# Attention inside an adaLN block: values in batches of two key blocks, a ring of twelve buffers, the maximum stream five ticks earlier, looser waits between additions

## The chip, the cores and the metric

The kernel runs on one core of a Trainium2 chip. The time is that of one execution on the device, in microseconds (us). The engines are PE (TensorE, with its weight loads as PEld), DVE (VectorE), ACT (ScalarE), POOL (GpSimd) and SP (which issues the transfers).

## The reference

Four sequences of 1024 tokens with 1024 features go through one transformer block with modulation. In float32 throughout:

```python
h = _layernorm(x) * (1 + ca) + sa
x = x + ga * attention(h, Wq, Wk, Wv, Wo)      # 32 query heads, 8 key/value heads of 32, RoPE, causal
h = _layernorm(x) * (1 + cb) + sb
x = x + gb * (h @ W.T + bias + lora(h))        # 8 LoRA pairs of rank 16, weighted
```

The change is in the attention alone: for each head, `softmax(q k^T / sqrt(32))` with a causal mask, times v.

## The kernel before

The program has four stages after one another: the modulation vectors, the projections to q, k and v (stored to HBM), the attention, and the second half (output projection, residual, norm, linear layer with LoRA folded into the weights). The attention stage runs from about 711 us to 2092 us.

**Groups.** The attention works on 32 groups (4 sequences times 8 key/value heads, `NG`), each with 4 query heads. For a group PE computes the scores twice. The first time (`max_scores`) they stand with the query on the partition, in 38 units (`MAX_UNITS`, `NM`), and DVE takes the negated row maximum of each (`take_max`). When all 38 are there, DVE joins and splits them into a high and a low part (`split_max`: L806, L811, L813), PE transposes the result (`turn`, L920), ACT copies it, and SP writes the rows by DMA below the query vectors in `q_stack`. So the second scores (`scores`) come out with the maximum already subtracted, with the key on the partition, in 20 units (`EXP_UNITS`, `NE`). ACT takes the exponential of each (`exp`, L756). The unit of key block 0 goes into `p_sum`, the others go into one of the buffers of a ring (`p_ring`).

**Quads.** One or two units hold one block of 128 keys for all four heads: a quad, of which a group has 12, four of them in half 0 (queries 0 to 511) and eight in half 1. `values(n, q)` multiplies the quad of probabilities by v on PE. It uses a quarter of the array for each head, and the four matmuls, one per head, run side by side (the trace counts each as two).

**Sums.** POOL adds the ring buffers into `p_sum` in place (`add`, L851; 15 additions in a group, `POOL_ADDS`: four in half 0, eleven in half 1). The first addition of a half may begin once the values of its first quad are done (`FIRST_QUAD`), since those matmuls read `p_sum` themselves. PE then sums `p_sum` over the partitions (`sums`, L930 and L935), which waits for the additions of its half.

**The order.** `group_steps` writes the order of all engines by hand, in 20 ticks for a group: each tick has one unit of scores, two or three max units of the next group (38 within ticks 0 to 15, by `max_ticks`), and a quad of values two ticks after its last unit (`LAG`). The turn is at tick 17, the sums of half 0 at tick 12, those of half 1 at tick 6 of the next group. Every engine goes through the same list in order.

**Buffers.** The max units, turns and sums share three banks of PSUM (`MS`, `wait_bank`): each waits until the third before it has been taken. The scores have two buffers (`SS`), the values one (`ctx_ps`). An exponential into a ring buffer waits until the probabilities that lay there have been used by the values and by the addition (8 buffers before).

Two lines of `add` set what an addition waits for besides its probabilities:

```python
pool.wait_ge(s_pv.sem, s_pv.at(NQ * n + FIRST_QUAD[hf] + 1))
if place:
    pool.wait_ge(s_ap.sem, s_ap.at(place))      # the addition just before
```

Of the kernel before, what the change touches and what calls it, by code (L numbers as in the profile page):

```python
# [35 lines left out]
NG = B * KV  # L36
# [10 lines left out]
EXP_UNITS = []  # L47
# [6 lines left out]
NE = len(EXP_UNITS)  # L54
# [11 lines left out]
POOL_ADDS = [u for u in RING_UNITS if u not in VECTOR_ADDS + TAIL[0] + TAIL[1]]  # L66
NV, NP = len(VECTOR_ADDS), len(POOL_ADDS)
# [12 lines left out]
NM = len(MAX_UNITS)  # L80
WIDE = [i for i in range(TT) if P * (i + 1) > HALF]

RING = 8
BATCH = 1
QS = 3
SS, MS = 2, 3
LAG = 2
SUM_AT = {1: 6, 0: 12}
TURN_AT = 17


def max_ticks():

    ticks, left = [[] for _ in range(NE)], list(range(NM))
    for t in range(NE):
        for _ in range(2 if t < 10 else 3):
            if left and t < TURN_AT:
                ticks[t].append(left.pop(0))
    assert not left
    return ticks  # L100


MAX_TICKS = max_ticks()


def group_steps(n):


    steps = []
    for u in range(NE):  # L110
        if n < NG:
            steps.append(("scores", n, u))
        if n + 1 < NG:
            steps += [("max", n + 1, m) for m in MAX_TICKS[u]]
        for hf in range(2):
            at = n - 1 if hf else n
            if u == SUM_AT[hf] and 0 <= at < NG:
                steps.append(("sum", at, hf))
        if n + 1 < NG and u == TURN_AT:
            steps.append(("turn", n + 1))  # L120
        at, v = (n, u - LAG) if u >= LAG else (n - 1, u - LAG + NE)
        if 0 <= at < NG and v == QUADS[QUAD_OF[v]][-1] and QUAD_OF[v] % BATCH == BATCH - 1:
            steps += [("values", at, q) for q in range(QUAD_OF[v] - BATCH + 1, QUAD_OF[v] + 1)]
    return steps


STEPS = [("max", 0, m) for m in range(NM)] + [("turn", 0)] + [s for n in range(NG + 1) for s in group_steps(n)]
SMALL = [s for s in STEPS if s[0] in ("max", "turn", "sum")]
BANK = {s: i % MS for i, s in enumerate(SMALL)}
BEFORE = {s: SMALL[i - MS] if i >= MS else None for i, s in enumerate(SMALL)}  # L130
# [474 lines left out]
def attention(nc, consts, qk_in, v_in, ctx_out, sums_out):  # L605


    with ExitStack() as ctx:
        def sb(name, shape, dt=F32):
            return ctx.enter_context(nc.sbuf_tensor(name, shape, dt))  # L610
# [4 lines left out]
        acc = sb("p_sum", [P, 2, 2, G, HALF])  # L615
        ring = sb("p_ring", [P, RING, 2 * HALF])
        cf = sb("ctx_raw", [P, 2, HALF])
# [14 lines left out]
        def count(name, step=1):  # L632
            return Count(nc, ctx, name, step)
# [8 lines left out]
        s_av, s_ap = count("probs_added_dve"), count("probs_added_pool")  # L642
# [4 lines left out]
        def ring_place(g, u):  # L647

            r = NR * g + RING_UNITS.index(u)
            before = r - RING  # L650
            return r % RING, None if before < 0 else (before // NR, RING_UNITS[before % NR])

        def probs(g, u):

            hf, j, hs, lo, n = EXP_UNITS[u]
            if j == 0:
                return acc[:, g % 2, hf, hs[0]:hs[-1] + 1, :]
            v = ring[:, ring_place(g, u)[0], :]
            if n > 256:
                return v.rearrange("p (h n) -> p h n", h=2)[:, :, 0:n]  # L660
            return v[:, 0:G * n].rearrange("p (h n) -> p h n", h=G)
# [14 lines left out]
        def _(sp):  # L676
            def load_v(b):
                if b >= 2:
                    sp.wait_ge(s_pv.sem, s_pv.at(NQ * KV * (b - 1)))
                sp.dma_start(V[:, b % 2, :, :], v_in[b].rearrange("(i p) d -> p i d", p=P)).then_inc(s_v[b % 2].sem, 16)  # L680
# [31 lines left out]
            load_v(0)  # L712
            for step in STEPS:
                kind, n = step[0], step[1]
# [16 lines left out]
        def _(act):  # L731
# [45 lines left out]

            for step in STEPS:
                kind, n = step[0], step[1]
# [10 lines left out]
        def _(dve):  # L790
# [34 lines left out]

            for step in STEPS:
                kind, n = step[0], step[1]
# [9 lines left out]
        @block.gpsimd  # L837
        def _(pool):
            nc.gpsimd.memset(ks[MHI:MHI + DH, :, :].bitcast(F32), 1.0).then_inc(init.sem, 1)

            def add(n, u):
                hf, j, hs, lo, w = EXP_UNITS[u]
                place = NP * n + POOL_ADDS.index(u)
                pool.wait_ge(s_ex.sem, s_ex.at(NE * n + u + 1))
                pool.wait_ge(s_pv.sem, s_pv.at(NQ * n + FIRST_QUAD[hf] + 1))
                if place:
                    pool.wait_ge(s_ap.sem, s_ap.at(place))
                if hs[-1] == G - 1 and VECTOR_DONE[hf]:
                    pool.wait_ge(s_av.sem, s_av.at(NV * n + VECTOR_DONE[hf]))
                a = acc[:, n % 2, hf, hs[0]:hs[-1] + 1, lo - hf * HALF:HALF]  # L850
                nc.gpsimd.tensor_tensor(a, a, probs(n, u), ALU.add).then_inc(s_ap.sem, 1)  # L851

            for step in STEPS:
                if step[0] == "values":
                    for u in QUADS[step[2]]:
                        if u in POOL_ADDS:
                            add(step[1], u)

        @block.tensor
        def _(pe):  # L860
# [77 lines left out]

            for step in STEPS:
                kind, n = step[0], step[1]  # L940
# [455 lines left out]
```

## Time and profile before

| | |
|---|---|
| median of 3 runs | 2926.89 us (2926.59 to 2929.13) |
| the profiled execution | 2926.28 us, span 2924.5 us |
| PE busy over the span | 2654.2 us (91%) |
| POOL, DVE, ACT busy | 1669.8, 1641.4, 1024.9 us |
| turn of group 1 to turn of group 31 | 781.71 to 2045.47 us |

The span is the time between the first and the last instruction in the trace; the execution's own time is 1.8 us more. A row of the timeline gives start, duration, engine, line and operation, and in brackets how long the engine was idle before it and what released it. The granted clock ("PEclk") is a share of 2.4 GHz: 1.00 is 2.4 GHz, 0.50 is 1.2 GHz. Durations of matmuls include the way through the array, so what one costs is best read from the start of one row to the start of the next.

### The profile page before, as it was taken

The numbers are of one execution on the slowest core, as the hardware profiler recorded it, in microseconds if no ns is written. First come the engines' busy times: TensorE is split into PE (matmuls) and PEld (weight loads), VectorE is DVE, ScalarE is ACT, GpSimd is POOL, SyncE is SP. The second block draws the span as 40 slices with busy tenths as digits, with TensorE's granted clock in tenths as the row PEclk, the third lists the DMA queues.
The fourth block names the chain that finished last, engine by engine and source line by source line (L and its number), as shares of the span: only waits on it lengthen the run. The fifth ranks groups of instructions, "written<-read, shape, count | busy, mean of one in ns | idle before, by whom it ended". The sixth has DMA issues, their size and how long they took to land. (4 is left out here: it accounts for less than half of the span.)

```text
span 2924.5 us, 37728 instructions
## 1 busy us (share of the span) xinstructions
PE 2654.2 (91%) x14588; PEld 1891.7 (65%) x14588; DVE 1641.4 (56%) x2483; ACT 1024.9 (35%) x1320; POOL 1669.8 (57%) x869
## 2 busy tenths in 40 slices
PE   2599999997999999999999999999559999999998
PEld 0378888885555555555555555555358878888887
DVE  2466666655566666665665666566134545455553
ACT  0333333321445545554554445444321111111111
POOL 0443333331577778777877877777515555455543
PEclk8799999997799999999999999999779999999999
DMA  9433333324222222222132212220252333333330
GB/s 347 143 128 113 115 112 109 112 80 126 63 66 58 70 67 54 70 70 67 45 80 70 67 40 70 70 61 18 77 173 80 94 109 95 100 108 94 108 97 34
DMA packets 178696, 267.55 MB, mean 91 GB/s; under 512 B 12197, under 2 KB 105509, under 8 KB 178393
## 3 DMA queue, kind: packets, MB, share of 16 engines
q1 hardware_dynamic: 178520, 265.13, 30.8%
q8 instruction: 120, 1.97, 0.3%
q14 instruction: 56, 0.45, 0.1%
HBM read 183.19 MB, written 80.84 MB: 90 GB/s over the span
## 5 line engine op out<-in xcount | busy, mean ns | idle before, releaser
L851 POOL TENSOR_TENSOR p_sum<-p_sum,p_ring 128x1024 f32<-128x1024 f32 (+2 forms) x480 | 1033.0, 2152 | 354.4 <-PE ctx_ps L912 284.3
L800 DVE TENSOR_REDUCE neg_max<-scores_q 128x1 f32<-128x512 f32 (+3 forms) x1216 | 729.8, 656 | 512.9 <-PE scores_q L894 327.3
L756 ACT ACTIVATE p_ring<-scores 128x1024 f32<-128x1024 f32 (+2 forms) x512 | 459.3, 917 | 405.4 <-PE scores L880 282.6
L894 PE MATMUL scores_q<-k_stack,q_stack 96*128 96x512 f32 (+3 forms) x1536 | 472.7, 387 | 4.1
L876 PE MATMUL scores<-q_stack,k_stack 98*128 98x512 f32 (+1 forms) x1216 | 438.8, 439 | 5.0 <-DMA q_stack<-neg_max_rows 4.9
L876 PEld LDWEIGHTS scores<-q_stack,k_stack 98*128 98x128 f32 x1216 | 197.4, 196 | 302.1 <-issue 172.2
L894 PEld LDWEIGHTS scores_q<-k_stack,q_stack 96*128 96x128 f32 x1536 | 281.1, 195 | 74.0 <-DVE neg_max L800 45.3
L579 PE MATMUL proj_ps<-h_hi,w_hi 128*128 128x512 f32 x768 | 304.8, 397 | 1.5 <-POOL h_lo L529 1.5
L579 PE MATMUL proj_ps<-h_hi,w_lo 128*128 128x512 f32 x768 | 300.3, 391 | 0.0
L579 PE MATMUL proj_ps<-h_lo,w_hi 128*128 128x512 f32 x768 | 300.1, 391 | 0.0
L536 POOL TENSOR_TENSOR roped_hilo<-roped_hilo 128x512 fp32r<-128x512 f32 x80 | 104.1, 1302 | 333.3 <-ACT roped_hilo L418 333.3
L912 PE MATMUL ctx_ps<-p_ring,v 128*32 128x512 f32 (+3 forms) x2560 | 280.7, 513 | 0.0
L1261 POOL TENSOR_TENSOR h_scaled<-h_scaled,mod_now 128x512 f32<-128x512 f32 x64 | 65.4, 1042 | 351.8 <-DVE h_scaled L1215 351.8
L1286 PE MATMUL po<-wo_hi,ctx_hi 128*128 128x512 f32 x512 | 204.1, 399 | 5.6 <-DVE wo_lo L1206 5.6
L1327 PE MATMUL pf<-we_hi,h_hi 128*128 128x512 f32 x512 | 200.4, 391 | 5.8 <-POOL h_lo L1265 5.8
L1286 PE MATMUL po<-wo_lo,ctx_hi 128*128 128x512 f32 x512 | 200.9, 392 | 0.0
L1286 PE MATMUL po<-wo_hi,ctx_lo 128*128 128x512 f32 x512 | 200.7, 392 | 0.0
L1327 PE MATMUL pf<-we_lo,h_hi 128*128 128x512 f32 x512 | 200.2, 391 | 0.0
L1327 PE MATMUL pf<-we_hi,h_lo 128*128 128x512 f32 x512 | 200.2, 391 | 0.0
L756 ACT ACTIVATE p_sum<-scores 128x1024 f32<-128x1024 f32 x128 | 131.0, 1024 | 142.3 <-PE scores L880 82.1
L898 PE MATMUL scores_q<-mask_q_k,ident_r 128*128 128x128 f32 x768 | 174.6, 227 | 0.0
L406 ACT COPY proj_raw<-proj_ps 128x512 f32<-128x512 f32 x96 | 56.2, 586 | 333.4 <-PE proj_ps L579 333.4
(130 smaller groups left out, 3844.9 us busy)
## 6 DMA issues: line engine op xcount, KB each, us to landing
q_stack<-qk_t SPq DMA_DIRECT2D x96, 512.0 KB, 6.9
qk_t<-roped_hilo SPq DMA_DIRECT2D x80, 512.0 KB, 2.8
wm<-in_L_wmod SPq DMA_DIRECT2D x12, 2048.0 KB, 19.9
x_in<-in_L_attn_resid SPq DMA_DIRECT2D x32, 512.0 KB, 6.4
ctx_t<-ctx_raw SPq DMA_DIRECT2D x64, 256.0 KB, 2.0
ctx_tile<-ctx_t SPq DMA_DIRECT2D x32, 512.0 KB, 4.0
inv_sums<-inv_t SPq DMA_DIRECT2D x128, 128.0 KB, 5.4
x_tile<-in_L_attn_resid SPq DMA_DIRECT2D x32, 512.0 KB, 3.3
```

Source lines behind the costliest of these rows:

```text
L536: nc.gpsimd.tensor_tensor(lo, lo.bitcast(F32), qst[r % QST][:, 0, :].bitcast(F32), ALU.subtract).then_inc(s_rl.sem, 1)
L579: last = nc.tensor.matmul(pps[e % PPS][:, :], w[a][:, c, k, :], h[m % 2][i][:, k, :], start=(k == 0 and n == 0), stop=(k == DC - 1 and n = ...
L756: nc.scalar.activation(probs(n, u), src, ACT.Exp, scale=SM_SCALE).then_inc(s_ex.sem, 1)
L800: nc.vector.tensor_reduce(negm[:, lo // HALF, hs[0]:hs[-1] + 1, i:i + 1], src, AX.X, ALU.max, negate=True).then_inc(s_mx.sem, 1)
L851: nc.gpsimd.tensor_tensor(a, a, probs(n, u), ALU.add).then_inc(s_ap.sem, 1)
L876: last = nc.tensor.matmul(o[a], ks[0:KS, n % QS, j * P:(j + 1) * P], qs[0:KS, n % QS, h0:h0 + per, lo:lo + w], start=True, stop=not diag)
L894: last = nc.tensor.matmul(dst[:, a, :], qs[0:MHI, n % QS, h, i * P:(i + 1) * P], ks[0:MHI, n % QS, lo:lo + w], start=not first, stop=not d ...
L898: last = nc.tensor.matmul(dst[:, a, w - P:w], identr[:, :], maskS[:, 0, :], start=False, stop=True)
L912: last = nc.tensor.matmul(cps[DH * h:DH * (h + 1), lo - hf * HALF:HALF], V[:, b % 2, j, g * DH:(g + 1) * DH], p[:, a, :], start=(j == 0), ...
L1261: nc.gpsimd.tensor_tensor(v, v, cur[:, 4 * h:4 * h + 4, 1:2].broadcast_to([P, 4, P]), ALU.add).then_inc(s_hf.sem, 1)
L1286: last = nc.tensor.matmul(po[h][:, :], cs[slot][a][:, k, :], wo[w][:, k, h * HALF:(h + 1) * HALF], start=(k == 0 and n == 0), stop=(k == D ...
L1327: mm = nc.tensor.matmul(pf[h][:, :], hs[a][:, k, :], we[w][:, k, h * HALF:(h + 1) * HALF], start=(k == 0 and n == 0), stop=(k == DC - 1 an ...
```

## The change

The ring has 12 buffers for 8. Values come in batches of two quads (`BATCH = 2`): both when the later one is due. The maximum stream is spread evenly over 20 ticks and begins five ticks earlier, so that the first ten units of a group's stream stand in ticks 15 to 19 of the group two before: group n+2 starts its maxima while group n still computes scores. An addition waits for the last earlier addition that touches one of its heads in the same half, and no longer for the one just before.

```diff
-RING = 8
-BATCH = 1
+RING = 12
+BATCH = 2
 QS = 3
 SS, MS = 2, 3
 LAG = 2
 SUM_AT = {1: 6, 0: 12}
+AHEAD = 5
 TURN_AT = 17
-def max_ticks():
-    ticks, left = [[] for _ in range(NE)], list(range(NM))
-    for t in range(NE):
-        for _ in range(2 if t < 10 else 3):
-            if left and t < TURN_AT:
-                ticks[t].append(left.pop(0))
-    assert not left
-    return ticks
-MAX_TICKS = max_ticks()
+MAX_TICK = [m * NE // NM - AHEAD for m in range(NM)]
...
-        if n + 1 < NG:
-            steps += [("max", n + 1, m) for m in MAX_TICKS[u]]
+        for at, t in ((n + 1, u), (n + 2, u - NE)):
+            if at < NG:
+                steps += [("max", at, m) for m in range(NM) if MAX_TICK[m] == t]
...
-STEPS = [("max", 0, m) for m in range(NM)] + [("turn", 0)] + [s for n in range(NG + 1) for s in group_steps(n)]
+STEPS = [("max", 0, m) for m in range(NM)] + [("turn", 0)] + [("max", 1, m) for m in range(NM) if MAX_TICK[m] < 0]
+STEPS += [s for n in range(NG + 1) for s in group_steps(n)]
...
-                place = NP * n + POOL_ADDS.index(u)
+                place = POOL_ADDS.index(u)
+                same = [p for p in range(place) if EXP_UNITS[POOL_ADDS[p]][0] == hf and set(EXP_UNITS[POOL_ADDS[p]][2]) & set(hs)]
                 pool.wait_ge(s_ex.sem, s_ex.at(NE * n + u + 1))
                 pool.wait_ge(s_pv.sem, s_pv.at(NQ * n + FIRST_QUAD[hf] + 1))
-                if place:
-                    pool.wait_ge(s_ap.sem, s_ap.at(place))
+                if same:
+                    pool.wait_ge(s_ap.sem, s_ap.at(NP * n + same[-1] + 1))
```

In the rows below, `scores` is the second computation, `scores_q` the max units (or the turn, where it reads `neg_max_hilo`), and `ctx_ps` the values. PE before, from the last two max units of tick 15 to the turn in tick 17 and the values behind it:

```order
L894 MATMUL scores_q<-k_stack,q_stack 128x512
L898 MATMUL scores_q<-mask_q_k,ident_r 128x128
L894 MATMUL scores_q<-k_stack,q_stack 128x512
L898 MATMUL scores_q<-mask_q_k,ident_r 128x128
L912 MATMUL ctx_ps<-p_ring,v 32x512 x4
L876 MATMUL scores<-q_stack,k_stack 128x384 x2
L880 MATMUL scores<-mask_k_q,ident_r 128x128 x2
L876 MATMUL scores<-q_stack,k_stack 128x384 x2
L880 MATMUL scores<-mask_k_q,ident_r 128x128 x2
L920 MATMUL scores_q<-consts,neg_max_hilo 128x128
L912 MATMUL ctx_ps<-p_ring,v 32x512 x4
```

Between the group's last max unit and its turn stand one quad of values and two units of scores, and no other max unit. After the change, from the values of tick 15 to the turn:

```order
L905 MATMUL ctx_ps<-p_ring,v 32x512 x8
L869 MATMUL scores<-q_stack,k_stack 128x384 x2
L873 MATMUL scores<-mask_k_q,ident_r 128x128 x2
L887 MATMUL scores_q<-k_stack,q_stack 128x256
L891 MATMUL scores_q<-mask_q_k,ident_r 128x128
L887 MATMUL scores_q<-k_stack,q_stack 128x256
L891 MATMUL scores_q<-mask_q_k,ident_r 128x128
L887 MATMUL scores_q<-k_stack,q_stack 128x384
L891 MATMUL scores_q<-mask_q_k,ident_r 128x128
L869 MATMUL scores<-q_stack,k_stack 128x384 x2
L873 MATMUL scores<-mask_k_q,ident_r 128x128 x2
```

Then come two more max units and the turn. The last max unit of the turned group now stands in tick 14, and six units of the group after it stand between that and the turn.

The additions of half 1 on POOL, with the semaphores that each waits for; before:

```order
L851 TENSOR_TENSOR p_sum<-p_sum,p_ring 128x1024 [waits probs_added_pool,values_done,probs_ready] x8
L851 TENSOR_TENSOR p_sum<-p_sum,p_ring 128x2x384 [waits probs_added_pool,values_done,probs_ready] x2
L851 TENSOR_TENSOR p_sum<-p_sum,p_ring 128x4x256 [waits probs_added_pool,values_done,probs_ready]
L851 TENSOR_TENSOR p_sum<-p_sum,p_ring 128x2x384 [waits probs_added_pool,values_done,probs_ready] x2
L851 TENSOR_TENSOR p_sum<-p_sum,p_ring 128x4x256 [waits probs_added_pool,values_done,probs_ready]
```

After:

```order
L844 TENSOR_TENSOR p_sum<-p_sum,p_ring 128x1024 [waits values_done,probs_ready] x2
L844 TENSOR_TENSOR p_sum<-p_sum,p_ring 128x1024 [waits probs_added_pool,values_done,probs_ready] x6
L844 TENSOR_TENSOR p_sum<-p_sum,p_ring 128x2x384 [waits probs_added_pool,values_done,probs_ready] x2
L844 TENSOR_TENSOR p_sum<-p_sum,p_ring 128x4x256 [waits probs_added_pool,values_done,probs_ready]
L844 TENSOR_TENSOR p_sum<-p_sum,p_ring 128x2x384 [waits values_done,probs_ready] x2
L844 TENSOR_TENSOR p_sum<-p_sum,p_ring 128x4x256 [waits probs_added_pool,values_done,probs_ready]
```

The order of the additions is the same. The two additions of one key block no longer wait for each other, and the semaphore value that the others wait for is that of the addition two before.

## Rows read from the trace of the kernel before

**Rows 1.** The page: the span, and the engines' busy time.
```profile
span 2924.5 us, 37728 instructions
PE 2654.2 (91%) x14588; PEld 1891.7 (65%) x14588; DVE 1641.4 (56%) x2483; ACT 1024.9 (35%) x1320; POOL 1669.8 (57%) x869
```

**Rows 2.** Windows from turn to turn: length, busy PE, PEld, DVE, ACT, POOL, clock, DMA.
```profile
1202.07:1245.46 43.39, 40.82 (x255) 23.91 (x256) 26.02 (x41) 21.08 (x25) 32.26 (x15) 0.93 0.25 59
1287.69:1328.38 40.69, 38.13 (x255) 23.11 (x255) 26.00 (x41) 21.07 (x25) 32.30 (x15) 0.99 0.26 64
```

**Rows 3.** Timeline of PE: the turns of groups 1 and 31.
```profile
781.71 0.47 PE L920 MATMUL scores_q<-consts,neg_max_hilo 128*128 128x128 f32 x1 [2.24 <-DVE neg_max_hilo L813]
...
2045.47 0.33 PE L920 MATMUL scores_q<-consts,neg_max_hilo 128*128 128x128 f32 x1 [2.25 <-DVE neg_max_hilo L813]
```

**Rows 4.** Timeline of PE: the values behind a turn at 1328.38.
```profile
1328.79 1.94 PE L912 MATMUL ctx_ps<-p_ring,v 128*32 128x512 f32 x8
```

**Rows 5.** Waits, window 740 to 2040: total us, times, longest.
```profile
PEld scores_q L894 <- DVE neg_max L800: 41.1, 123, 0.4
```

**Rows 6.** Timeline of PE at full clock, 1298 to 1309.
```profile
1298.11 1.07 PE L912 MATMUL ctx_ps<-p_sum,v 128*32 128x512 f32 x8
1299.11 0.73 PE L876 MATMUL scores<-q_stack,k_stack 98*128 98x512 f32 x2
...
1303.15 0.63 PE L894 MATMUL scores_q<-k_stack,q_stack 96*128 96x512 f32 x2
1303.71 1.07 PE L930 MATMUL scores_q<-p_sum,ones_v 128*32 128x512 f32 x8
...
1306.89 0.43 PE L912 MATMUL ctx_ps<-p_ring,v 128*32 128x128 f32 x8
1307.24 0.74 PE L876 MATMUL scores<-q_stack,k_stack 98*128 98x512 f32 x2
1307.82 0.63 PE L894 MATMUL scores_q<-k_stack,q_stack 96*128 96x512 f32 x2
1308.29 0.63 PE L876 MATMUL scores<-q_stack,k_stack 98*128 98x512 f32 x2
1308.76 0.40 PE L894 MATMUL scores_q<-k_stack,q_stack 96*128 96x512 f32 x1
```

**Rows 7.** Timeline of PE: the end of the last group.
```profile
2073.87 1.62 PE L912 MATMUL ctx_ps<-p_ring,v 128*32 128x384 f32 x24
2089.23 1.08 PE L930 MATMUL scores_q<-p_sum,ones_v 128*32 128x512 f32 x4 [13.74 <-POOL p_sum L851]
```

**Rows 8.** Timeline of DVE: the split without additions beside it, and with them.
```profile
736.60 0.19 DVE L813 TENSOR_TENSOR neg_max_hilo<-neg_max,neg_max_hilo 128x32 fp32r<-128x32 f32 x1
...
1242.11 0.77 DVE L806 TENSOR_TENSOR neg_max<-neg_max 128x16 f32<-128x16 f32 x1
...
1243.13 2.27 DVE L813 TENSOR_TENSOR neg_max_hilo<-neg_max,neg_max_hilo 128x32 fp32r<-128x32 f32 x1
```

**Rows 9.** Timeline of POOL beside that split.
```profile
1243.02 2.34 POOL L851 TENSOR_TENSOR p_sum<-p_sum,p_ring 128x1024 f32<-128x1024 f32 x1 [0.17 <-POOL p_sum L851]
```

**Rows 10.** Timeline of DVE in the second half of the program, near 2407.
```profile
2407.09 2.48 DVE L1169 TENSOR_TENSOR x_tile<-x_tile,gated 128x512 f32<-128x512 f32 x1
```

**Rows 11.** Timeline of POOL beside it.
```profile
2406.64 2.39 POOL L1240 TENSOR_TENSOR ctx_tile<-ctx_tile,inv_sums 128x1024 f32<-128x1024 f32 x1
2408.98 2.85 POOL L1273 TENSOR_TENSOR x_tile<-x_tile,gbias 128x1024 f32<-128x1024 f32 x1
```

**Rows 12.** Timeline of PE: a turn, and the next group's first scores.
```profile
953.18 0.33 PE L920 MATMUL scores_q<-consts,neg_max_hilo 128*128 128x128 f32 x1 [2.26 <-DVE neg_max_hilo L813]
...
957.44 0.73 PE L876 MATMUL scores<-q_stack,k_stack 98*128 98x512 f32 x2 [0.80 <-DMA q_stack<-neg_max_rows]
```

**Rows 13.** Groups of instructions by shape, POOL's additions, window 740 to 2040.
```profile
L851 POOL TENSOR_TENSOR p_sum<-p_sum,p_ring 128x1024 f32<-128x1024 f32 x306 | 725.3, 2370 | 154.7 <-PE ctx_ps L912 108.4 <-POOL p_sum L851 46.4
L851 POOL TENSOR_TENSOR p_sum<-p_sum,p_ring 128x768 f32<-128x768 f32 x122 | 222.6, 1825 | 190.9 <-PE ctx_ps L912 175.5 <-POOL p_sum L851 15.2 <-ACT p_ring L756 0.2
```

## The prediction

> **What bounds the kernel now.** I read the page first, then PE's timeline over a few groups, then the waits, and last POOL and DVE beside PE's stalls. The page shows PE busy for 91% of the span and POOL, next, for 57% [rows 1]. In the attention PE is the bound too: a group from turn to turn has PE busy for 40.82 of 43.39 us, POOL for 32.26, DVE for 26.02 and ACT for 21.08 [rows 2]. The change touches nothing outside this stage, so what counts is the length of a group. From the turn of group 1 to that of group 31 it is (2045.47 - 781.71) / 30 = 42.13 us [rows 3]. Three things in it are not matmul work.
>
> First, each turn finds PE idle for 2.25 us, waiting for the last instruction of DVE's split [rows 3]. Second, in most groups the clock falls at that stall. The values behind the turn at 1328.38 take 1.94 us where the same eight matmuls take 1.07 at another place [rows 4, 6]. A group with a mean clock of 0.99 takes 40.69 us, one with 0.93 takes 43.39 [rows 2]. So the falls cost 42.13 - 40.69 = 1.44 us a group in the mean. Third, PE waits for a bank that DVE hasn't emptied: 41.1 us over 1300 us, or 30.9 groups, which makes 1.33 us a group [rows 5].
>
> **The change, part by part.**
>
> *The turn.* Before, one quad of values and two units of scores lie between the last max unit and the turn. After, PE has a pair of quads, three units of scores and six max units there. Nearly all the 2.25 us of idleness should go, and with it the reason for the clock to fall. I take off 2.25 and 1.44.
>
> *The new place of that wait.* DVE's queue is in order: the first six maxima of the next group stand behind the split. The fourth of these units on PE needs the bank of the first, so it waits until DVE has split and then taken one maximum, and the turn needs the bank of the fourth. DVE needs about 0.8 us for the last maximum of the old group with its start (busy 26.0 us less 3.2 us of split, over 38 maxima, is 0.6 each [rows 2, 8]), about 3.4 us for the split if it ends with the second boundary of the additions as it does now [rows 8, 9], and 0.6 us for the first new maximum: 4.8 us. PE meanwhile has the scores of tick 15, three max units, two quads of values and the scores of tick 16. The values are 1.85 us (below). The rest is some 4900 columns, at 0.47 us for 1024 columns (1307.82 to 1308.29 [rows 6]) 2.25 us, and nearer 3 since its pieces are small: 4.1 to 4.9 us. So PE waits 0 to 0.7 us there, and again a little at the turn. I take 0.75 us together, between 0 and the whole 2.25 of today.
>
> *The bank waits.* The even stream has at most two max units in a tick where there were three. PE needs 0.94 us for the smallest tick (scores and two units, 0.47 us each [rows 6]) and DVE 1.2 us for its two maxima, with three banks as slack and a pair of values every few ticks. I take off 1.33 and put 0.2 back; the ends are 0 and all of it.
>
> *Two quads in one go.* A narrow block costs more than its columns. Eight matmuls of 512 columns take 1.00 us to the next start, of 128 columns 0.35 us [rows 6]. The difference gives 4 x 128 columns = 0.217 us, so the fixed part is 0.35 - 0.217 = 0.13. Ahead of a narrow block the two max units take 0.56 us (1303.15 to 1303.71), against 0.47 without one behind them: 0.09 more. The scores after values take 0.58 us (1307.24 to 1307.82), after max units 0.47: 0.11 more [rows 6]. So entering and leaving the narrow form costs 0.33 us. Does the second quad really ride free? At the end of the last group three quads (384, 256 and 128 columns) run together in 1.62 us, end of the last one included, where 768 columns alone are 1.30 [rows 7]. Each fixed part beyond the first is gone there. There are 12 blocks of values and 2 of sums in a group, and the sums of half 1 touch a block of values, so 13 blocks. After, there are 6 and 2, none touching: 8. Five fewer are 5 x 0.33 = 1.65 us. The bounds are 0 (the second quad isn't free) and 2.0 (six).
>
> *The additions.* Their 0.17 us gaps [rows 9] go within a key block and perhaps altogether, some 2 us a group on POOL. POOL isn't the bound, so this pays nothing by itself. But the batch makes half 1's additions start two ticks later (tick 11 for 9). These are nine of 2.37 us and two of 1.82 [rows 13], 25.0 us, and begin about 1.2 us after the pair of values does. PE needs the result at tick 6 of the next group, 15 of 20 ticks later, more than 27 us even at 36 us a group. That leaves a slack of 1 to 2.5 us. With half 0's additions POOL is busy for 32.3 us a group [rows 2] and stays below PE.
>
> *The ring.* Each exponential now waits for the addition 12 units earlier. That addition lies at least eight ticks back, so I cost it at nothing. With 8 buffers the later values would have come near the edge.
>
> *The transfer of the maxima.* From a turn to the first scores that had to wait for its DMA it takes 4.26 us [rows 12]. After the change PE has two units of scores, four max units and two quads between them, some 4.5 us. Cost nothing, bound 0.5.
>
> *The ends.* Ten max units of group 1 now stand ahead of group 0's scores. They overlap the wait for the first rows of maxima, and are missing at the other end, where ACT and POOL set the pace: PE waits 13.74 us for the last additions [rows 7]. Half 1's later start lengthens this tail by 1 to 2 us. I add 1 us in all, bounds -3 and +6.
>
> **The sum.** 40.69 - 2.25 - 1.33 + 0.20 - 1.65 + 0.75 = 36.41 us a group at full clock, against 42.13: 5.72 less. Over 30 groups that is 171.6, less 1 at the ends. The profiled execution took 2926.3 us, which stands 0.6 under the median of the runs shown, so 2926.3 - 170.6 = 2755.7; I say **2755**.
>
> **The rivals.**
>
> *DVE is passed over.* The split has two instructions with both inputs in SBUF. L813 takes 0.19 us with no addition beside it, and 2.27 with one; it starts at 1243.13 and ends at 1245.40, just after the addition that began at 1243.02 and ended at 1245.36 [rows 8, 9]. So DVE waits for the addition's end and slips into the 0.17 us gap behind it. The change takes such gaps away. If POOL's next addition goes ahead of a waiting DVE, the split starves until the row of ten additions ends (22.6 us after it began), and needs the end of one more. It would be done some 26 us after the values instead of 11: 15 us more of PE's time in a group, 450 in all, **3206**. It decides from the third addition on which DVE is passed over (2.37 us each against 5.7 saved). Against it: in the program's second half POOL runs without a gap, L1240 ends at 2409.0 and L1273 starts at 2408.98. DVE's L1169 waited since 2407.09 and ended at 2409.57, and L1273 took 2.85 us where L1240 of the same size took 2.39 [rows 10, 11]. There the waiting DVE got in and POOL paid. The Trainium skill, "SBUF — State Buffer", section "SBUF: two separate sides", calls this pair of ports an exclusive lock which whichever instruction starts first holds to its end; taken alone, this rule lets a gapless POOL start first each time, which is this rival. The rows show the other outcome at one kind of boundary. Chance 0.05.
>
> *The split misses a boundary.* The phase between split and additions is new. If the last maximum comes just after a boundary, the split takes one more addition, 2.3 us, and PE waits for it: 38.7 us a group, **2825**. Chance 0.12.
>
> *The batch brings nothing*, since the block is drained between quads: 38.1 us, **2805**. Rows 7 speak against it. Chance 0.05.
>
> *The clock goes on falling* at the shorter stalls: 37.85 us, **2799**. For it: the clock fell at stalls of 2.25 us. Against: one of these groups kept 0.99 with such a stall [rows 2]. Chance 0.08.
>
> *POOL comes late* for the sums of half 1: the slack is small, and DVE's turns at the port lengthen additions. With 1.5 us of waiting, 37.9 us and **2801**. Chance 0.06.
>
> **How the numbers follow.** My forecast has the remaining 0.64, and a range of its own of 2728 (no new wait and half of a sixth block: 0.92 us a group less) to 2789 (the bank waits stay: 1.13 more). The four rivals at 2799 to 2825 are within reach of a range of 2728 to 2828, which leaves out the starving split and a double mishap. About 0.2% of the time, 6 us, is what a measurement can tell from none. Faster by more than that holds for all but the first rival: 0.94; within it 0.01; slower 0.05.
>
> **What would show it.** In the new profile the wait of the turn for the split should be nearly gone, the clock at 0.99 or more through the attention, the turns 36.4 us apart, and sixteen matmuls in one piece of values at 1.7 us plus 0.13. DVE's waits on bank should sit at the fourth max unit of a new group. L813 should still take one addition (2.3 us), with an addition beside it some 0.2 us longer than the others. I would be wrong if L806 or L813 took over 3 us, if the sums of half 1 waited for POOL, or if the exponentials waited for it.

## The result and the profile after

The changed kernel is slower: 3059.78 us in the median of four executions, against 2926.74 before, a ratio of 1.043 (95% interval 1.036 to 1.049). Its own executions lie far apart, 3033.17, 3055.16, 3064.40 and 3150.19 us, where those of the kernel before lie within 5.2 us. Both seem to have one cause, as will be seen. An execution over 1.5% above the fastest of its kernel is left out of the ratios: here the one of 3150.19 us, in e8 the one of 3160.37, and in e4 one of 3646.75 whose clock was 0.648 in the mean. The profiled execution is the fastest of the four, 3033.17 us.

The page of the changed kernel, the lines that answer to [rows 1], with the clock in 40 slices and the line of an instruction that wasn't among the costly ones before:

```profile
span 3031.3 us, 37724 instructions
PE 2618.5 (86%) x14588; PEld 1972.0 (65%) x14588; DVE 1875.9 (62%) x2483; ACT 1028.6 (34%) x1320; POOL 1655.4 (55%) x869
...
PEclk8799999995999898898888988898979999999999
...
L798 DVE TENSOR_TENSOR neg_max<-neg_max 128x16 f32<-128x16 f32 x32 | 247.0, 7718 | 1.1
```

PE is less busy, DVE is 234 us busier with the same 2483 instructions, and 247.0 us of DVE are the 32 joins (L798, which was L806), 7718 ns each in the mean, where one took 0.77 us before [rows 8]. The clock is lower in the attention: 0.88 in the mean from the turn of group 1 to that of group 31, against 0.96 before. The windows from turn to turn, to be read beside [rows 2] (length, busy PE, PEld, DVE, ACT, POOL, clock, DMA):

```profile
956.17:997.24 41.07, 38.56 (x257) 26.38 (x256) 28.90 (x42) 21.20 (x25) 31.90 (x16) 0.92 0.28 63
997.24:1047.36 50.12, 38.52 (x257) 26.33 (x256) 37.98 (x42) 21.22 (x25) 36.91 (x18) 0.84 0.22 52
```

There are two kinds of groups. Of the 30 periods between the turns of groups 1 and 31, 14 are short (40.9 us in the mean) and 16 long (49.9 us). The mean is 45.7, against 42.13 before [rows 3]: 30 x 3.58 = 107.4 us, the whole difference of the profiled executions (3033.17 - 2926.28 = 106.9).

DVE's timeline in a short group:

```profile
905.71 1.10 DVE L798 TENSOR_TENSOR neg_max<-neg_max 128x16 f32<-128x16 f32 x1
906.84 2.31 DVE L803 CAST neg_max_hilo<-neg_max 128x32 fp32r<-128x32 f32 x1
909.18 2.29 DVE L805 TENSOR_TENSOR neg_max_hilo<-neg_max,neg_max_hilo 128x32 fp32r<-128x32 f32 x1
```

And in a long one:

```profile
1028.93 14.40 DVE L798 TENSOR_TENSOR neg_max<-neg_max 128x16 f32<-128x16 f32 x1
1043.37 0.18 DVE L803 CAST neg_max_hilo<-neg_max 128x32 fp32r<-128x32 f32 x1
1043.59 0.19 DVE L805 TENSOR_TENSOR neg_max_hilo<-neg_max,neg_max_hilo 128x32 fp32r<-128x32 f32 x1
```

POOL's timeline beside the long one:

```profile
1022.95 20.35 POOL L844 TENSOR_TENSOR p_sum<-p_sum,p_ring 128x1024 f32<-128x1024 f32 x9 [2.68 <-PE ctx_ps L905]
1047.42 1.82 POOL L844 TENSOR_TENSOR p_sum<-p_sum,p_ring 128x768 f32<-128x768 f32 x1 [4.12 <-ACT p_ring L748]
```

Nine additions (eight of 128x1024 and one of 128x768, in one row) run without a gap from 1022.95 to 1043.30. The join was due at 1028.93 and ended at 1043.33, together with the last of them. POOL then had nothing left: it next waited 4.12 us for an exponential. PE's timeline shows why (the fourth new max unit, in the short and in the long group):

```profile
912.31 0.69 PE L887 MATMUL scores_q<-k_stack,q_stack 96*128 96x384 f32 x1 [2.51 <-DVE neg_max L792]
...
1044.63 0.69 PE L887 MATMUL scores_q<-k_stack,q_stack 96*128 96x384 f32 x1 [11.60 <-DVE neg_max L792]
```

PE stood for 11.60 us waiting for the bank of the first new maximum, which lay behind the split in DVE's queue. So no further scores were made, no exponentials followed, and POOL ran dry. Only then did DVE get in. The waits of the changed kernel, window 740 to 2140 (total us, times, longest):

```profile
PE scores_q L887 <- DVE neg_max L792: 220.9, 30, 11.9
```

Even the short groups gain little. With no gap to slip into, the join takes the rest of one addition and the cast and the subtraction one addition each: 5.7 us for the split where it took 3.2. PE waits 2.5 us, and the clock still falls behind it (0.92 over that group).

### The profile page after: what moved, and what is told of

Its sections match the earlier page's. It is cut to its first block and busy times, and to the rows that moved or that the text cites. A ratio compares the mean times of both kernels' runs of the same rounds, so it can differ in the third digit from the quotient of the medians.

```text
span 3031.3 us, 37724 instructions
## 1 busy us (share of the span) xinstructions
PE 2618.5 (86%) x14588; PEld 1972.0 (65%) x14588; DVE 1875.9 (62%) x2483; ACT 1028.6 (34%) x1320; POOL 1655.4 (55%) x869
## 5 line engine op out<-in xcount | busy, mean ns | idle before, releaser
L844 POOL TENSOR_TENSOR p_sum<-p_sum,p_ring 128x1024 f32<-128x1024 f32 (+2 forms) x480 | 1019.2, 2147 | 477.6 <-PE ctx_ps L905 382.8
L792 DVE TENSOR_REDUCE neg_max<-scores_q 128x1 f32<-128x512 f32 (+3 forms) x1216 | 741.9, 658 | 386.5 <-PE scores_q L891 228.2
L887 PE MATMUL scores_q<-k_stack,q_stack 96*128 96x512 f32 (+3 forms) x1536 | 508.3, 406 | 220.9 <-DVE neg_max L792 220.9
L887 PEld LDWEIGHTS scores_q<-k_stack,q_stack 96*128 96x128 f32 x1536 | 306.3, 211 | 264.5 <-DVE neg_max L792 229.6
L869 PE MATMUL scores<-q_stack,k_stack 98*128 98x512 f32 (+1 forms) x1216 | 446.9, 447 | 2.0 <-ACT p_ring L748 2.0
L869 PEld LDWEIGHTS scores<-q_stack,k_stack 98*128 98x128 f32 x1216 | 211.4, 207 | 153.6 <-issue 97.4
L798 DVE TENSOR_TENSOR neg_max<-neg_max 128x16 f32<-128x16 f32 x32 | 247.0, 7718 | 1.1
L905 PE MATMUL ctx_ps<-p_ring,v 128*32 128x512 f32 (+3 forms) x2560 | 232.7, 472 | 0.0
L891 PE MATMUL scores_q<-mask_q_k,ident_r 128*128 128x128 f32 x768 | 188.1, 245 | 0.0
```

The lines of the kernel that those rows point to most:

```text
L792: nc.vector.tensor_reduce(negm[:, lo // HALF, hs[0]:hs[-1] + 1, i:i + 1], src, AX.X, ALU.max, negate=True).then_inc(s_mx.sem, 1)
L798: nc.vector.tensor_tensor(both[0], both[0], both[1], ALU.min).then_inc(s_mc.sem, 1)
L869: last = nc.tensor.matmul(o[a], ks[0:KS, n % QS, j * P:(j + 1) * P], qs[0:KS, n % QS, h0:h0 + per, lo:lo + w], start=True, stop=not diag)
L887: last = nc.tensor.matmul(dst[:, a, :], qs[0:MHI, n % QS, h, i * P:(i + 1) * P], ks[0:MHI, n % QS, lo:lo + w], start=not first, stop=not d ...
L891: last = nc.tensor.matmul(dst[:, a, w - P:w], identr[:, :], maskS[:, 0, :], start=False, stop=True)
L905: last = nc.tensor.matmul(cps[DH * h:DH * (h + 1), lo - hf * HALF:HALF], V[:, b % 2, j, g * DH:(g + 1) * DH], p[:, a, :], start=(j == 0), ...
```

## The experiments

Two theories were stated first. **G**: the 0.17 us gaps between additions let DVE's split in, and the looser waits took them away. **O**: the new order, the batch or the ring shifts the split against the additions, and the waits play no part. The first four runs each have one part of the change alone, or all but one.

**e1: the changed kernel with the old waits.**

```diff
-                place = POOL_ADDS.index(u)
-                same = [p for p in range(place) if EXP_UNITS[POOL_ADDS[p]][0] == hf and set(EXP_UNITS[POOL_ADDS[p]][2]) & set(hs)]
+                place = NP * n + POOL_ADDS.index(u)
...
-                if same:
-                    pool.wait_ge(s_ap.sem, s_ap.at(NP * n + same[-1] + 1))
+                if place:
+                    pool.wait_ge(s_ap.sem, s_ap.at(place))
```

> The changed kernel with one part undone: each addition waits for the one just before it again. Theory G (the 0.17 us gaps between additions are what lets DVE's split in; without them it is passed over until POOL runs out of probabilities): the join L798 never takes over 2.4 us (16 of 32 took 14.4 in the changed kernel), the split is 3.2 us again, the turns are 36.4 to 37.5 us apart, 2755 to 2795 us. Rival O (the new order or the batch shifts the split against the additions, and the waits play no part): still some groups of 50 us, 3000 us or more. Rival C (the clock): the groups without starvation stay near 41 us, 2890 us.

Measured: 2776.42 us, 0.949 of before (0.947 to 0.950). Every join took 1.5 us, every split 4.0 us (DVE's timeline, one group, and POOL's beside it):

```profile
1105.51 1.50 DVE L798 TENSOR_TENSOR neg_max<-neg_max 128x16 f32<-128x16 f32 x1
1107.04 0.18 DVE L803 CAST neg_max_hilo<-neg_max 128x32 fp32r<-128x32 f32 x1
1107.26 2.30 DVE L805 TENSOR_TENSOR neg_max_hilo<-neg_max,neg_max_hilo 128x32 fp32r<-128x32 f32 x1
```

```profile
1104.59 2.39 POOL L843 TENSOR_TENSOR p_sum<-p_sum,p_ring 128x1024 f32<-128x1024 f32 x1 [0.17 <-POOL p_sum L843]
1107.14 2.37 POOL L843 TENSOR_TENSOR p_sum<-p_sum,p_ring 128x1024 f32<-128x1024 f32 x1 [0.17 <-POOL p_sum L843]
```

The join ends at 1107.01, in the gap between 1106.98 and 1107.14, and the cast begins in the same gap. The turns are 36.85 us apart in the mean, most of them 36.7, at full clock (window of one such group, columns as above):

```profile
1185.00:1221.70 36.70, 35.83 (x256) 23.73 (x256) 26.94 (x42) 21.23 (x26) 32.40 (x16) 1.00 0.30 70
```

PE waits for the fourth max unit's bank for 0.81 us. No group is as long as 41 us: O and C both fall. The three other parts of the change are thus worth 5% together, and the waits alone turn that into a loss of 4%.

**e2: the kernel before with the looser waits alone** (the same lines, the other way).

> The kernel before with the looser waits alone. Theory G: the join, the cast and L813's subtraction each wait for the end of an addition at best, so the stall at the turn grows from 2.25 us to about 4.7, and in some groups DVE is passed over until POOL has nothing left, some 5 to 8 us more: 2980 to 3150 us. Rival O: nothing to see, within 0.5% of 2927 us.

Measured: 3099.93 us, 1.060 of before (1.058 to 1.061), and here every group is alike: joins of 7.87 us, turns 47.78 us apart. A turn in PE's timeline:

```profile
1216.79 0.47 PE L921 MATMUL scores_q<-consts,neg_max_hilo 128*128 128x128 f32 x1 [7.28 <-DVE neg_max_hilo L813]
```

The stall of 2.25 us [rows 3] has become 7.28. POOL had ten additions in a row from 1194.07 to 1216.25 and then waited 5.59 us for an exponential; the join, due at 1208.42, ended at 1216.29. Theory O falls: nothing of the order was changed here.

**e3: the earlier maximum stream alone.**

```diff
-RING = 12
-BATCH = 2
+RING = 8
+BATCH = 1
```

in e1's kernel.

> The kernel before with the earlier and even maximum stream alone (ring of 8, single quads, old waits). By the terms of the prediction: 42.13 - 2.25 (stall) - 1.44 (clock) - 1.1 (bank waits) + 0.75 = 38.1 us a group, 2805 us. If the clock falls at whatever stalls are left, 39.5 us, 2848 us. If a ring of 8 is too small for it, ACT waits for additions and the gain is gone.

Measured: 2818.11 us, 0.963 of before (0.962 to 0.965), 38.37 us a group for 38.1 expected. No turn but the first and the last finds a stall, and PE waits 0.86 us a group at the fourth max unit (25.8 us over 30).

**e4: the batch and the ring alone.**

```diff
-RING = 8
-BATCH = 1
+RING = 12
+BATCH = 2
```

in the kernel before.

> The kernel before with two quads in one go and the ring of twelve alone (old maximum stream, old waits). By the term of the prediction five fewer narrow blocks of 0.33 us: 42.13 - 1.65 = 40.5 us a group, the stall of 2.25 us at the turn as before, 2877 us. If quads in one go save nothing: 2927 us.

Measured: 2829.54 us, 0.967 of before (0.965 to 0.969), 38.71 us a group: 3.4 us less where 1.65 was expected. The waits of this kernel, window 740 to 2040:

```profile
PE scores_q L920 <- DVE neg_max_hilo L813: 30.6, 31, 1.0
PE scores L876 <- DMA q_stack<-neg_max_rows: 14.5, 32, 3.2
```

The stall at the turn is 1.0 us instead of 2.25, since two quads instead of one lie ahead of it, and its join happens to meet a gap (0.32 us). In the profiled execution the clock didn't fall at a stall so short: all 30 groups have 1.00. 42.13 - 1.65 - 1.25 - 1.44 is 37.8 us. The rest to 38.7 is in part a new wait for the rows of maxima: the first row of the next group's scores finds them late, by about 0.3 us in most groups. I had priced the batch without the stall that it shortens.

**e5: one gap put back** in the changed kernel.

```diff
+                if u == 13:
+                    same = [place - 1]
                 if same:
                     pool.wait_ge(s_ap.sem, s_ap.at(NP * n + same[-1] + 1))
```

> The changed kernel with one gap put back: of the ten additions of half 1 that run back to back, the sixth (unit 13) alone waits for the one just before it. It begins 11.7 us after the first, and the join is asked for 6.0 us after the first. Theory G: in the groups where the join is passed over it ends at that gap, so it takes 5.7 to 6.2 us instead of 14.4, never more; L805 behind it takes 2.3 us, or is passed over in its turn until POOL has nothing left. 2930 to 3050 us. If gaps play no part, joins of 14.4 us are still there.

Measured: 2939.57 us, 1.005 of before (1.002 to 1.007). DVE's and POOL's timelines in one group:

```profile
1024.84 5.76 DVE L798 TENSOR_TENSOR neg_max<-neg_max 128x16 f32<-128x16 f32 x1
1030.64 0.18 DVE L803 CAST neg_max_hilo<-neg_max 128x32 fp32r<-128x32 f32 x1
1030.85 2.27 DVE L805 TENSOR_TENSOR neg_max_hilo<-neg_max,neg_max_hilo 128x32 fp32r<-128x32 f32 x1
```

```profile
1030.74 10.52 POOL L846 TENSOR_TENSOR p_sum<-p_sum,p_ring 128x1024 f32<-128x1024 f32 x5 [0.17 <-POOL p_sum L846]
```

The join ends at 1030.60, in the one gap of 0.17 us, and its 5.76 us lie in the 5.7 to 6.2 expected. Of the 31 joins with additions beside them, 23 took 5.76 us and 8 took 1.10; none took more. This is the closest to a proof of G: one semaphore wait on one addition moved the join's end from the end of POOL's work to that wait.

**e6: the split without the shared port**, in the changed kernel with its looser waits. All four instructions are reductions, each with one operand in SBUF; `pair` is a new buffer, and `neg_max` is set to 3e38 once.

```diff
...
-                both = [negm[:, s, :, WIDE[0]:] for s in range(2)]
-                nc.vector.tensor_tensor(both[0], both[0], both[1], ALU.min).then_inc(s_mc.sem, 1)
...
-                nc.vector.tensor_copy(mhl[:, 0:G * TT], flat).then_inc(s_mh.sem, 1)
...
-                nc.vector.tensor_tensor(mhl[:, G * TT:2 * G * TT], flat, mhl[:, 0:G * TT].bitcast(F32), ALU.subtract
-                                        ).then_inc(s_ml.sem, 1)
+                both = negm[:, :, :, :].rearrange("p s h i -> p (h i) s")
+                nc.vector.tensor_reduce(pair[:, 0, :].bitcast(F32), both, AX.X, ALU.min).then_inc(s_mc.sem, 1)
+                nc.vector.tensor_reduce(pair[:, 1, :], both, AX.X, ALU.min, negate=True).then_inc(s_mc.sem, 1)
...
+                nc.vector.tensor_reduce(mhl[:, 0:G * TT], both, AX.X, ALU.min).then_inc(s_mh.sem, 1)
...
+                    nc.vector.tensor_reduce(mhl[:, G * TT:2 * G * TT],
+                                            pair[:, :, :].bitcast(F32).rearrange("p s k -> p k s"),
+                                            AX.X, ALU.add).then_inc(s_ml.sem, 1)
```

> The changed kernel, its looser waits kept, with the join and the split written as four reductions that read one SBUF operand each (min over the two halves; the same negated and rounded; the same rounded; the sum of the first two): the same values, no instruction with two SBUF inputs and no cast. Theory G with the port as the cause: each of the four takes under 0.3 us beside running additions, none is passed over, PE's wait at the fourth max unit is gone, 36.0 us a group, 2740 to 2770 us. If DVE is held up by additions whatever it reads, it stays at 3000 us and more.

Measured: 2730.94 us, 0.934 of before (0.933 to 0.936), faster than both kernels and 9 us below the range expected. The groups by line, window 740 to 2040:

```profile
L805 DVE TENSOR_REDUCE neg_max_pair<-neg_max 128x32 f32<-128x64 f32 x31 | 6.8, 221 | 1.1
L806 DVE TENSOR_REDUCE neg_max_pair<-neg_max 128x32 fp32r<-128x64 f32 x31 | 6.5, 210 | 0.0
L812 DVE TENSOR_REDUCE neg_max_hilo<-neg_max_pair 128x32 fp32r<-128x64 f32 x31 | 6.5, 210 | 0.0
L809 DVE TENSOR_REDUCE neg_max_hilo<-neg_max 128x32 fp32r<-128x64 f32 x31 | 6.5, 209 | 0.0
```

Each takes 0.21 us whatever POOL does. The window over the whole attention up to the last turn, and one of a single group:

```profile
740.00:1835.00 1095.00, 1094.96 (x7798) 733.08 (x7801) 732.64 (x1293) 648.24 (x764) 970.88 (x455) 0.99 0.31 74
...
1185.00:1220.50 35.50, 35.50 (x257) 23.67 (x257) 23.75 (x42) 21.19 (x25) 32.04 (x16) 1.00 0.31 73
```

PE has next to no idle time (0.04 us of 1095), and a group takes 35.4 us.

**e7: the same split in the kernel before.**

> The kernel before with the split written as four reductions. The split takes 0.8 us instead of 3.2, so the turn finds no stall, and the clock has no reason to fall: 42.13 - 2.25 - 1.44 = 38.4 us a group, 2815 us. If the port isn't the cause of the 2.27 us: 2927 us.

Measured: 2840.9 us, 0.972 of before (0.968 to 0.975), 39.1 us a group for 38.4. The stall at the turn is gone. The 0.7 us that are missing are PE's wait for the maxima rows' transfer, 0.65 us in nearly every group (24.8 us over the window, 3.2 of them ahead of group 0). ACT copies the turned maxima 1.02 us after the turn instead of 0.37 to 0.51, because it is still at an exponential when the turn comes; before, it ended that one during the stall. One group took 44.0 us: its clock fell behind a wait of 1.17 us for that transfer.

**e9: a ring of 8** in e1's kernel (`RING = 8`).

> The changed kernel with the old waits (which took 2776 us) and a ring of 8 buffers instead of 12. By the order each exponential then waits for an addition and for values that lie at least three ticks back: no wait of ACT on POOL or on values appears, within 0.5% of 2776 us. If the batch needs the larger ring: ACT waits for POOL, 2800 us or more.

Measured: 2775.3 us against e1's 2776.42, both 0.949 of before (e9: 0.948 to 0.951). ACT waits for POOL ten times, 3.1 us in all, where none was expected. The ring of twelve isn't needed for two quads in one go.

**e8 and e10: the join asked for later.** What decides whether a waiting join is passed over? The expectations below start from times rounded to 10 ns: of the changed kernel's joins all ten asked for 1.27 or 1.28 us into an addition were passed over, all five at 1.30 weren't, of sixteen at 1.31 six were. That looked like a threshold. To the nanosecond, as the trace holds them, they are three kinds that don't mix: ten at 1.276 to 1.278 us, passed over; fifteen at 1.304 or 1.305, let in at the next boundary; six at 1.307 or 1.308, passed over. These runs add one or five unused reductions ahead of the join (shown for one, in part):

```diff
+                for i in range(1):
+                    nc.vector.tensor_reduce(idle[:, i, :], negm[:, :, :, :].rearrange("p s h i -> p (h i) s"),
+                                            AX.X, ALU.min).then_inc(s_idle.sem, 1)
...
+                dve.wait_ge(s_idle.sem, s_idle.at(1 * (n + 1)))
```

> The changed kernel with one small reduction (0.2 us, its result unused) ahead of each join. In the changed kernel the join is asked for 1.27 to 1.31 us into an addition of 2.34; all ten asked for at 1.27 or 1.28 were passed over, all five at 1.30 got in at the next boundary, and those at 1.31 were mixed; a kernel that asks at 0.33 is passed over every time. Theory P (the moment within the addition decides, and from about 1.3 us on DVE gets in): asked at 1.5 to 1.6 us, no join takes over 2.5 us in any group, turns some 41 us apart, 2880 to 2910 us. Rival R (chance at each join): about half of the groups still have joins of 14 us, 3000 us or more.

> The changed kernel with five such reductions ahead of each join, so that it is asked for about 1.1 to 1.3 us later, near a boundary or just behind it. Theory P: asked just ahead of a boundary it gets in at once; asked 0.1 to 0.3 us into the next addition it is like the joins asked for at 0.33 us, passed over in every group, joins of some 12 us, 3150 us or more. Rival R: about half of the groups, 3000 to 3100 us.

Measured: e8 3125.9 us (two executions, 3091.43 and 3160.37), e10 3147.82 us (3146.84 and 3148.80). The joins' rows in the groups by line, e8 first:

```profile
L809 DVE TENSOR_TENSOR neg_max<-neg_max 128x16 f32<-128x16 f32 x32 | 413.8, 12931 | 1.1
```

```profile
L809 DVE TENSOR_TENSOR neg_max<-neg_max 128x16 f32<-128x16 f32 x32 | 369.8, 11555 | 1.1
```

In e8's profiled execution, the longer one, 29 of 31 joins were passed over (14.15 us, one 15.89) and two took 0.86; in e10 27 were (13.6) and four took 0.35. They were asked for 1.53 to 1.59 and 2.04 to 2.10 us into an addition. Theory P falls for e8, which should have had none, and for e10, whose joins were asked for ahead of a boundary and should have got in at once. A join asked for just behind a boundary wasn't tested. Rival R, half of the groups, fits neither trace. That the shift changed the share isn't shown: the changed kernel's longest execution, 3150.19 us, is as long as these, and e8's other one is 69 us shorter than its profiled one.

**e11: reductions and old waits together.**

> The changed kernel with the split as four reductions (2731 us) and the old waits between additions. POOL isn't the bound, and with nothing of DVE at the port the gaps matter to nobody: within 0.3% of 2731 us, 35.4 us a group. If the looser waits are worth something of their own once the port is free: 2740 us or more.

Measured: 2731.01 us, 0.935 of before (0.933 to 0.936), 35.41 us a group. With DVE off the port, the looser waits neither cost nor gain.

## Why the prediction was wrong

The forecast was 2755 us (2728 to 2828), faster at 0.94; it came out at 3060. The step that failed is the price of the looser waits: nothing in the prediction, 6% alone. By the steps of the prediction:

- *What bounds the kernel*, the stall and the clock: right. e7 took the stall away by the reductions alone, and the groups went from 42.13 to 39.1 us with the clock at 1.00 in 29 of 30.
- *The additions*: this is the step that failed. "Their 0.17 us gaps go ... POOL isn't the bound, so this pays nothing by itself." I costed the edit at nothing, from POOL's side. Its price was on DVE. Alone it costs 6% (e2); undone in the changed kernel, the time is 2776 us (e1).
- *The new place of the wait*: right in place, and with the old waits also in size, 0.83 us a group (24.9 us over 30 in e1) for 0.75. The 3.4 us for the split rested on the gaps, while the same prediction took them away. Without them even the lucky groups have 5.7 us, because the cast needs an addition's end too. I had counted the cast at its 0.18 us and not asked why it was so short.
- *The batch*: the second quad rides free, as said; sixteen matmuls of 512 columns took 1.86 us from start to start (1029.92 to 1031.78), predicted 1.7 + 0.13. From e3 to e1 it is worth 1.5 us a group, predicted 1.65. From the kernel before it is worth 3.4 (e4), because it also shortens the stall.
- *The bank waits, the transfer, the ring*: the sum for a group was 36.41; e1 has 36.85 in the mean and 36.7 in most groups (in three the clock fell). The bank waits of [rows 5], 41.1 us, are 0.2 us in e6; in e1 what is left of them, 29.5 us, is the wait at the fourth max unit. PE doesn't wait for the transfer in e1. The ring cost nothing and, by e9, does nothing.
- *The ends*: 1 us predicted. From the last turn to the end of the span it is 879.0 us before, 889.2 in e1 and 885.3 in e6: 10 and 6 us more. What lies ahead of the turn of group 1 took 781.7, 781.7 and 779.6. That part was undersized, in e1 beyond its bound of 6.
- *The rivals*: "DVE is passed over" is what happened, with its mechanism, its place and its sign, in 16 of the 31 joins of the profiled execution. The other three executions were 22 to 117 us longer; at 9.0 us for each join passed over (49.9 - 40.9) that makes, as an estimate, 18 to 29 of 31. L806 over 3 us was named as a sign of being wrong, and the page shows it. I gave it 0.05. Its price a group was predicted as 15 us on top of 36.4; the long groups have 49.9, 13.5 more. PE's wait accounts for 10.8 of them (11.6 us for 0.8); the rest goes with a clock of 0.84 to 0.88, which I had not counted. The wait ends sooner than I said because PE's stall starves POOL in its turn.
- *The evidence against the rival* was one boundary in another stage [rows 10, 11], where DVE got in. It was true and proved too little: the changed kernel shows both outcomes at joins that were asked for within 4 ns of one another (1.304 and 1.308 us into an addition). The rule that I quoted from the Trainium skill ("SBUF — State Buffer", "SBUF: two separate sides"), that whichever starts first holds the port to its end, told more: without a gap POOL's next addition can start first every time. The trace agrees with it here, 14.40 us, while six further additions began.

What stays open is which of the two gets the port at a boundary without a gap. The cast and the subtraction, asked for 0.1 us into an addition, always got in at the next boundary (all 15 joins that weren't passed over); a join asked for at 0.33 us never did (e2); near 1.3 us 15 of 31 did, near 1.55 us two, near 2.07 us four. No moment within the addition decides by itself: 1.305 us let the join in in the changed kernel and not in e5 (whose joins at 1.279 to 1.307 us were all passed over and those at 1.328 and 1.329 all let in), and e10 has both outcomes at 2.092. Whether it matters that DVE had just held the port wasn't tried.

## What to carry to other kernels

Before loosening waits on GpSimd, look for VectorE instructions whose duration ends exactly in the gaps between GpSimd's: they live on those gaps, and a back-to-back stream can hold them off until it runs out of work. Better here than keeping the gaps (2776 us) was to keep the short, critical VectorE instructions off the shared port, as reductions (2731 us); four of 0.21 us replaced 3.2 to 14.8 us. And don't put a costly rival at 0.05 on the evidence of one row.

## What was not expected of the hardware

A VectorE instruction of 0.17 us of work was held off for 14.4 us, past six boundaries between additions (in e8 once for 15.9 us, past seven). The outcome differs between groups of one execution whose requests lie within 4 ns of one another, and that is probably why the kernel's time varies by 117 us from run to run (3033.17 to 3150.19; only the fastest has a trace). A cast from float32 to float32r with one SBUF operand is held off like the instructions with two (2.31 us for 0.18), while reductions of the same size aren't (0.21 us). And a stall of 1.0 us at every turn left the clock at its full level in all 30 groups of e4's profiled execution, where 2.25 us let it fall behind 20 of 30 turns in the kernel before.
